# Attention values summed one key tile at a time, and feed-forward weights folded from quarter pieces

## The chip, the core and the metric

The kernel runs on one NeuronCore of a Trainium2 chip. The metric is the device time of one execution in microseconds. Five engines run their own instruction streams and meet only at semaphores: PE (TensorE, matrix products), DVE (VectorE), ACT (ScalarE), POOL (GpSimd) and SP (here only a queue that issues DMAs). The profile lists the weight loads of PE apart, as PEld.

## What is computed

The reference is a small residual network over `x` of shape (2, 2048, 256), in four steps, each behind a layer norm:

```python
x = x + attn_a(layernorm(x))   # 44 fixed offsets back in time per token, softmax over them
x = x + ffn(layernorm(x))      # 8 groups of 512 tokens, each with weights of its own
x = x + attn_b(layernorm(x))   # full softmax attention, 16 heads of 16, rotary q and k
x = x + ffn(layernorm(x))      # the same 8 groups again

def ffn(x):                    # no activation between the two products
    h1 = einsum('gmh,goh->gmo', xg, W1) + b1
    return einsum('gmo,gho->gmh', h1, W2) + b2
def attn_b(x):                 # scores = q k^T / 4, attn = softmax(scores), out = attn v
    ...
```

Since nothing stands between the two products of the feed-forward step, W1 (1024x256) and W2 (256x1024) of a group can be multiplied into one 256x256 matrix and b1 into b2, once, and used twice.

## The kernel before

`build` runs four stages one after the other, each a block of its own that ends when all its engines and stores are through.

**fold_ffn (lines 75 to 158)** multiplies the weights of the 8 groups in float32. SP loads whole groups into one of two slots: W1 (1 MB, L102), W2 transposed (1 MB, L103), b1 (L104), b2 (L105); all four count on one semaphore, `loaded[s]`, and a slot is loaded again only when the group before in it is evacuated (`evac`, L101). PE waits for `loaded[s]`, does 16 products of 128x128 by 128x256 (two row blocks m, eight key blocks k; two records each, L118) and then, when DVE has weighted and summed W2 by b1 in eight steps (L134, L136), one product with a column of ones (L121). DVE copies the result out (L144, L145), and ACT stores it to `mt_d` and `bc_d` (L153, L154). Behind the loop ACT stores one more group into the unused place 0 (L156, L157) and waits for all stores. Every engine runs this as a loop of 4 turns with two slots in each.

**local_stage (lines 337 to 868)** is everything up to the queries, keys and values of attn_b. The change doesn't touch it.

**full_attention (lines 871 to 1193)** takes 4 heads and 512 queries at a time: 2 batches x 4 head groups x 4 query chunks make `ITERS` = 32 iterations. In iteration x PE computes transposed scores of 16 key tiles of 128 keys (`score`, L1047; 4 heads, so 64 scores of 128x512, n = 4 x tile + head). Each goes to one of 3 PSUM banks, in turn; ACT takes the exponential from there into `pr` (L1132), which holds 4 key tiles. A score waits until the exponential of the score three before is done (`bank_free`). PE then multiplies `pr` with the values (`weigh`, L1057): for a key tile 4 products of 128x32 by 128x512 in float32, one per head in its own 32 columns of the array, which run side by side and have two records each.

The exponentials need a bound on the scores of each query, taken one iteration ahead: `max_unit` (L1018) computes 128 queries by 1024 keys into one of two PSUM buffers (two matmuls), DVE takes the maximum (L1149). There are 32 of these units in an iteration; the last 12 of a set are done in the iteration before (`CARRY`). When a set is complete, DVE splits it into three bf16 parts (`max_parts`, L1151 to 1167), PE transposes them into a score bank (`max_rows`, L1027, before score 46), DVE copies them out (L1173) and SP writes them as three extra rows of `qs` (L937).

The order on PE is written out by hand, in pairs of key tiles (`PAIRS` = 8):

```python
for i in range(8):
    score(x, 8 * d + i, q, slot)
    if i in (0, 3, 5, 7):
        fill((0, 3, 5, 7).index(i))
...
weigh((d - 1) % PAIRS, (x - 1) * SCORES + 8 * d)
```

So a pair is 8 scores with 4 units between them, and then the 8 value products of the pair before, in one go. `weigh` counts `pv_done` once a pair. ACT waits for it before it overwrites `pr`; at n == 9 ACT also copies the finished output of the iteration before out of `ps_o` (`take_output`, L1122), and PE waits for this (`o_sb`) at d == 1, before the first value product of the new iteration. POOL waits for `pv_done` before it loads values (`load_v`) and queries and keys (`load_qk`) of later groups. Iterations 1 and 32 stand outside the loop over x, with constant addresses; iteration 32 has no units.

**final_stage (lines 1196 to 1356)** does the rest, chunk by chunk. The change doesn't touch it.

Of the kernel before, what the change touches and what calls it, by code (L numbers as in the profile page):

```python
# [74 lines left out]
def fold_ffn(nc, W1, W2T, b1, b2, mt_d, bc_d):  # L75

    OC = INTER // P
    with ExitStack() as ctx:
        sb = lambda n, s, d: ctx.enter_context(nc.sbuf_tensor(n, s, d))
        sem = lambda n: ctx.enter_context(nc.semaphore(n))  # L80
        w1 = sb("w1", [P, 2, OC, C], F32)
        w2 = sb("w2", [P, 2, OC, C], F32)
        b1s = sb("b1s", [P, 2, OC], F32)
        b2s = sb("b2s", [1, 2, C], F32)
# [5 lines left out]
        loaded = [sem("fold_loaded0"), sem("fold_loaded1")]  # L90
        mm_done, evac, stored = sem("fold_mm"), sem("fold_evac"), sem("fold_stored")
        start, weighted, acc_step = sem("fold_start"), sem("fold_weighted"), sem("fold_acc_step")
        block = ctx.enter_context(nc.Block())

        @block.sync
        def _(sp):
            with sp.Fori(0, NG // 2) as i:
                for s in range(2):
                    g = i * 2 + s

                    sp.wait_ge(evac, i * 2 + s + 1)  # L101
                    sp.dma_start(w1[:, s], W1[g].rearrange("(k p) n -> p k n", p=P)).then_inc(loaded[s], 16)  # L102
                    sp.dma_start(w2[:, s], W2T[g].rearrange("(k p) n -> p k n", p=P)).then_inc(loaded[s], 16)  # L103
                    sp.dma_start(b1s[:, s], b1[g]).then_inc(loaded[s], 16)  # L104
                    sp.dma_start(b2s[:, s], b2[g].unsqueeze(0)).then_inc(loaded[s], 16)  # L105

        @block.tensor
        def _(pe):
            pe.wait_ge(start, 1)
            pe.sem_inc(mm_done, 2)  # L110
            with pe.Fori(0, NG // 2) as i:
                for s in range(2):
                    pe.wait_ge(loaded[s], i * 64 + 64)

                    pe.wait_ge(evac, i * 2 + s + 1)
                    for m in range(KC):
                        for k in range(OC):
                            pe.matmul(ps[:, s, m, 0:C], w1[:, s, k, m * P:(m + 1) * P], w2[:, s, k, :],  # L118
                                      start=(k == 0), stop=(k == OC - 1))
                    pe.wait_ge(weighted, i * 2 + s + 1)  # L120
                    pe.matmul(ps[0:1, s, 2, 0:C], column[:, :], acc[:, s, :], start=True, stop=True).then_inc(mm_done, 1)  # L121

        @block.vector
        def _(dve):
            dve.memset(column[:, :], 1.0).then_inc(start, 1)
            dve.sem_inc(evac, 2)
            dve.sem_inc(stored, 64)
            with dve.Fori(0, NG // 2) as i:
                for s in range(2):

                    dve.wait_ge(loaded[s], i * 64 + 64)
                    for k in range(OC):
                        if k == 0:
                            step = dve.tensor_scalar(acc[:, s, :], w2[:, s, k, :], b1s[:, s, k:k + 1], None, ALU.mult)  # L134
                        else:
                            step = dve.scalar_tensor_tensor(out=acc[:, s, :], in0=w2[:, s, k, :], scalar=b1s[:, s, k:k + 1],  # L136
                                                            in1=acc[:, s, :], op0=ALU.mult, op1=ALU.add)
                        if k < OC - 1:
                            step.then_inc(acc_step, 1)
                            dve.wait_ge(acc_step, (i * 2 + s) * (OC - 1) + (k + 1))  # L140
                    step.then_inc(weighted, 1)
                    dve.wait_ge(mm_done, i * 2 + s + 3)
                    dve.wait_ge(stored, i * 64 + 64)
                    dve.tensor_copy(mt[:, s], ps[:, s, 0:KC, 0:C])  # L144
                    dve.tensor_tensor(bc[:, s], ps[0:1, s, 2, 0:C], b2s[:, s], ALU.add).then_inc(evac, 1)  # L145

        @block.scalar
        def _(act):
            with act.Fori(0, NG // 2) as i:
                for s in range(2):  # L150
                    g = i * 2 + s
                    act.wait_ge(evac, i * 2 + s + 3)
                    act.dma_start(mt_d[g + 1].rearrange("(k p) n -> p k n", p=P), mt[:, s]).then_inc(stored, 16)  # L153
                    act.dma_start(bc_d[g + 1].unsqueeze(0), bc[:, s]).then_inc(stored, 16)  # L154
# [3 lines left out]
            act.wait_ge(stored, 64 + 32 * NG + 32)  # L158
# [712 lines left out]
def full_attention(nc, D):  # L871
# [9 lines left out]
    CARRY = AHEAD * PER_PAIR  # L881
    ROWS_AT = 8 * (PAIRS - AHEAD) + 6
    SCORES = KT * GRP
    QK_LOADS = 16 * 6 * (1 + NCH)

    with ExitStack() as ctx:
        sb = lambda n, s, d: ctx.enter_context(nc.sbuf_tensor(n, s, d))
        sem = lambda n: ctx.enter_context(nc.semaphore(n))
        ps_s = ctx.enter_context(nc.psum_tensor("ps_s", [P, 3, CH], F32))
# [67 lines left out]
        def _(pool):  # L957
# [23 lines left out]
            def group(G, more_qk, more_v):  # L981

                if more_qk:
                    pool.wait_ge(pv_done, G * (NCH * PAIRS) + 1)
                    n = G + 3
                    load_qk(pool.snap(n // HG), pool.snap(n % HG), n)
                if more_v:
                    n = G + 1
                    b, g = pool.snap(n // HG), pool.snap(n % HG)
                    for first, last, loaded in V_LOADS:  # L990
                        pool.wait_ge(pv_done, G * (NCH * PAIRS) + ((NCH - 1) * PAIRS + last // 2))
                        load_v(b, g, first, last, loaded)
# [14 lines left out]
        def _(pe):  # L1007
# [22 lines left out]
            def bank_free(x, op):  # L1030

                if op < 3:
                    last = SCORES + 1 - (2, 1, 3)[op]
                    if not (isinstance(x, int) and x == 1):
                        pe.wait_ge(p_ready, (x - 1) * SCORES + (exps_before(last) + 1 - SCORES))
                elif op - 3 == ROWS_AT:
                    if not (isinstance(x, int) and x == ITERS):
                        pe.wait_ge(nmt_sb, x + 1)
                else:
                    pe.wait_ge(p_ready, (x - 1) * SCORES + (exps_before(op - 3) + 1))  # L1040

            def score(x, n, q, slot):
# [4 lines left out]
                pe.matmul(ps_s[:, op % 3, :],  # L1047
# [4 lines left out]
            def weigh(d, ready):  # L1052

                pe.wait_ge(p_ready, ready)
                for kt in (2 * d, 2 * d + 1):
                    for j in range(GRP):
                        mm = pe.matmul(ps_o[SLOT * j:SLOT * (j + 1), :], vg[:, kt, j, :], pr[:, kt % 4, j, :],  # L1057
                                       start=(kt == 0), stop=(kt == KT - 1), skip_group_check=True)
                mm.then_inc(pv_done, 1)

            def iteration(x, q, slot, group, sets, groups, first=False):

                pe.wait_ge(neg_ld, x * 16)
                for d in range(PAIRS):
                    ahead = d >= PAIRS - AHEAD
                    if sets and d == 0:
                        pe.wait_ge(qk_ready, groups[0])
                    if sets and d == PAIRS - AHEAD:
                        pe.wait_ge(qk_ready, groups[1])

                    def fill(e):
                        if sets:
                            i = PER_PAIR * d + e
# [363 lines left out]
```

## Time and profile before

| | us |
|---|---|
| median of 3 runs (2709.53 to 2711.10) | 2710.88 |
| the profiled execution, its own time | 2717.06 |
| its span in the trace | 2715.4 |
| fold_ffn, from 0 to the first load of local_stage | 93.9 |
| first score of the attention | 1032.2 |
| one iteration of the attention loop | 48.10 |
| last score product ends, last output copied | 2568.5 |

The stages follow each other, so a time saved in one is saved in the whole. Within a stage, the question is which engine's chain of waits sets its length. The page of the profile gives sums over the span; the timeline gives, for a window, each instruction's start and length, with runs of alike instructions merged (x8), and in brackets how long its engine had stood idle and for whom.

### The profile page before, as it was taken

What the parts mean: (1) busy time and instruction counts of PE and PEld (TensorE: products, weight loads), DVE (VectorE), ACT (ScalarE), POOL (GpSimd) and SP (SyncE); (2) the same over time, 40 slices, a digit from 0 to 9 for tenths busy, and PEclk for the clock granted to TensorE, in tenths of its full rate; (3) what the DMA queues carried; (4) which work ended last, traced back from release to release, by engine and by line L of the source; (5) the groups of instructions that cost most, each with busy time, mean ns of one, the idle gap of its engine ahead of it and who ended that gap; (6) DMA issues with size and microseconds to landing.
All of it is one profiled execution on the core that took longest, in us unless ns stands there. A gap on an engine that the chain in (4) does not pass through costs nothing. (4 is left out here: it accounts for less than half of the span.)

```text
span 2715.4 us, 48858 instructions
## 1 busy us (share of the span) xinstructions
PE 2449.6 (90%) x15112; PEld 971.3 (36%) x15112; DVE 2032.7 (75%) x2445; ACT 1418.2 (52%) x2704; POOL 725.0 (27%) x936
## 2 busy tenths in 40 slices
PE   7679999999997559999999999999999999999778
PEld 5334545455545202332333333233333333333144
DVE  4388989999995367787778778787777877877145
ACT  0133434444434105776676677677667767766601
POOL 0488777787772042002002011020000000000010
PEclk9889999999998758999999999999999999999989
DMA  7424444554454295004004013031000000000061
GB/s 220 152 56 120 119 120 120 138 138 118 131 131 132 74 141 64 5 10 59 2 16 52 2 32 36 4 49 17 4 18 4 10 10 4 10 12 2 18 180 44
DMA packets 244299, 174.94 MB, mean 64 GB/s; under 512 B 105172, under 2 KB 215141, under 8 KB 244197
## 3 DMA queue, kind: packets, MB, share of 16 engines
q1 hardware_dynamic: 212406, 116.05, 16.3%
q0 software_dynamic: 13216, 36.72, 9.1%
q10 hardware_dynamic: 18578, 20.85, 2.6%
q8 instruction: 61, 1.00, 0.2%
q14 instruction: 38, 0.31, 0.0%
HBM read 116.49 MB, written 48.31 MB: 61 GB/s over the span
## 5 line engine op out<-in xcount | busy, mean ns | idle before, releaser
L1149 DVE TENSOR_REDUCE mx<-ps_m 128x1 f32<-128x1024 f32 x1036 | 1211.7, 1221 | 327.9 <-PE ps_m L1018 324.6
L1132 ACT ACTIVATE pr<-ps_s 128x512 f32<-128x512 f32 x2048 | 1064.3, 618 | 535.5 <-PE ps_s L1047 520.3
L1047 PE MATMUL ps_s<-qs,ks 99*128 (+1 forms) x2048 | 709.3, 385 | 53.7 <-ACT pr L1132 21.0
L1018 PE MATMUL ps_m<-ks,qs 96*128 (+1 forms) x2072 | 639.0, 391 | 39.6 <-DMA qs<-q_d 33.0
L1057 PE MATMUL ps_o<-pr,vg 128*32 128x512 f32 x4096 | 493.8, 600 | 0.0
L1047 PEld LDWEIGHTS ps_s<-qs,ks 99*128 (+1 forms) x2048 | 196.7, 96 | 715.3 <-issue 619.5
L540 POOL TENSOR_TENSOR prod_p<-qT,kT 128x512 f32<-128x512 f32 x336 | 411.9, 1253 | 108.7 <-PE PSa L583 89.6
L975 POOL DMA_DIRECT2D vg<-vb_d x24 | 19.7, 822 | 1218.8 <-PE ps_o L1057 1211.0
L791 DVE TENSOR_TENSOR prod_d<-PSa,kT 128x512 f32<-128x512 f32 x368 | 232.9, 677 | 24.7 <-PE PSa L583 17.0
L1018 PEld LDWEIGHTS ps_m<-ks,qs 96*128 (+1 forms) x2072 | 180.6, 98 | 176.4 <-DVE mx L1149 44.1
L583 PE MATMUL PSa<-prod_p,sj 128*32 128x512 f32 x672 | 202.9, 618 | 8.7 <-DVE prod_d L791 6.8
L583 PE MATMUL PSa<-prod_d,sj 128*32 128x512 f32 x736 | 203.0, 618 | 8.0 <-DVE prod_d L791 3.1
L1057 PEld LDWEIGHTS ps_o<-pr,vg 128*32 128x32 f32 x4096 | 107.5, 109 | 261.0 <-issue 195.4
L742 ACT COPY a<-PSa 128x512 f32<-128x512 f32 x128 | 68.9, 588 | 185.5 <-PE PSa L641 185.3
L968 POOL DMA_DIRECT2D qs<-q_d x168 | 85.6, 513 | 15.9 <-issue 4.8
L118 PE MATMUL fold_ps<-w 128*128 128x256 f32 x256 | 65.0, 419 | 20.2 <-DMA b2s<-in_b 20.2
L641 PE MATMUL PSa<-ident,own 128*128 128x128 f32 x512 | 70.1, 281 | 6.6 <-DMA prev<-skew 4.1
L588 PE MATMUL PSa<-t_xm,wqkv_b 128*128 128x512 f32 x128 | 69.8, 696 | 5.2 <-DVE rope_b L848 3.6
L641 PEld LDWEIGHTS PSa<-ident,own 128*128 128x128 f32 x512 | 57.8, 143 | 38.6 <-issue 33.7
L555 POOL TENSOR_TENSOR far<-far,fart 128x128 f32<-128x128 f32 x128 | 66.0, 515 | 10.0
L194 ACT ACTIVATE f_sq<-f_xm 128x1024 f32<-128x1024 f32 x8 | 8.5, 1056 | 114.0 <-DVE f_xm L190 114.0
L588 PE MATMUL PSa<-h_xm,wqkv 128*128 128x512 f32 x128 | 65.2, 634 | 2.0 <-DVE h_xm L330 1.3
(134 smaller groups left out, 2073.4 us busy)
## 6 DMA issues: line engine op xcount, KB each, us to landing
own<-skew SPq DMA_DIRECT2D x64, 512.0 KB
ks<-k_d POOLq DMA_DIRECT2D x42, 256.0 KB, 9.3
qs<-q_d POOLq DMA_DIRECT2D x168, 64.0 KB, 9.5
skew<-attn SPq DMA_DIRECT2D x64, 164.0 KB, 4.2
w<-in_W SPq DMA_DIRECT2D x8, 1024.0 KB
w<-in_W2T SPq DMA_DIRECT2D x8, 1024.0 KB
vb_d<-vb SPq DMA_DIRECT2D x8, 1024.0 KB, 5.3
q_d<-qparts ACTq DMA_DIRECT2D x16, 384.0 KB, 2.7
```

The lines of the kernel that those rows point to most:

```text
L540: pool.tensor_tensor(prod_p[:, n % RING, :], qT[:, c, :], kT[:, c, col:col + CH], ALU.mult).then_inc(prod_p_ready, 1)
L583: pe.matmul(PS[SLOT * g:SLOT * (g + 1), SC_BANK, :], sj[:, BANK_J * bank + 4 * g + r, :], rhs[:, n % RING, :], start=(r == 0), stop=(r == ...
L588: mm = pe.matmul(out, weight[:, k, :], x[:, k, :], start=(k == 0), stop=(k == KC - 1))
L641: tr = pe.transpose(PS[:, TURN_BANK[half], h * P:(h + 1) * P], own[:, w % 2, 4 * half + h, :], ident[:, :])
L742: act.copy(a0[:, 4 * half:4 * half + 4, :], PS[:, TURN_BANK[half], :].rearrange("p (h t) -> p h t", h=4)).then_inc(turn_sb, 1)
L791: dve.tensor_tensor(prod_d[:, n % RING, :], PS[:, Q_BANK[c], :], kT[:, c, col:col + CH], ALU.mult).then_inc(prod_d_ready, 1)
L968: pool.dma_start(qs[r, bass.ds(g * NCH + n, 1), :, :].rearrange("p a j t -> p (a j) t"), D["q_d"][Q_STACK[i], :, heads, bass.ds(b * T + (1 ...
L1018: mm = pe.matmul(ps_m[:, u % 2, kc * CH:(kc + 1) * CH], qs[0:KROWS, bass.ds(nq, 1), j, qt * P:(qt + 1) * P].rearrange("p a t -> p (a t)"), ...
L1047: pe.matmul(ps_s[:, op % 3, :], ks[:, bass.ds(slot, 1), j, kt * P:(kt + 1) * P].rearrange("p a t -> p (a t)"), qs[:, bass.ds(q, 1), j, :]. ...
L1057: mm = pe.matmul(ps_o[SLOT * j:SLOT * (j + 1), :], vg[:, kt, j, :], pr[:, kt % 4, j, :], start=(kt == 0), stop=(kt == KT - 1), skip_group_ ...
L1132: act.activation(pr[:, n // GRP % 4, n % GRP, :], ps_s[:, op % 3, :], ACT.Exp, scale=HD ** -0.5).then_inc(p_ready, 1)
L1149: dve.tensor_reduce(mx[:, j * TILES + qt, half:half + 1], ps_m[:, u % 2, :], AX_X, ALU.max).then_inc(m_read, 1)
```

## The change

In `fold_ffn` the loops are written out and the weights arrive in pieces of a quarter group (2 of the 8 key blocks of W1 and of W2, 256 KB each). There are 8 places for pieces, each with its own semaphore. PE starts a group with its first piece; a place is loaded again when PE and DVE are both done with the piece in it. b1 and b2 of all groups are loaded once, behind the second piece, on a semaphore for DVE alone. DVE sums the weighting of group g before it copies group g - 1 out. The additional store into place 0 is gone.

```diff
+    PIECES = 4
+    KP = OC // PIECES
+    DEPTH = 8
@@ sync
+                if i >= DEPTH:
+                    sp.wait_ge(piece_used, i - DEPTH + 1)
+                    sp.wait_ge(weighted, i - DEPTH + 1)
+                sp.dma_start(w1[:, n], W1[g, rows, :].rearrange("(k p) n -> p k n", p=P)).then_inc(w_ld[n], 16)
+                sp.dma_start(w2[:, n], W2T[g, rows, :].rearrange("(k p) n -> p k n", p=P)).then_inc(w_ld[n], 16)
+            for i in range(NG * PIECES):
+                piece(i)
+                if i == 1:
+                    sp.dma_start(b1s[:, :, :], b1.rearrange("g p k -> p g k"), allow_slow_non_contiguous=True).then_inc(b_ld, 16)
+                    sp.dma_start(b2s[:, :, :], b2.unsqueeze(0)).then_inc(b_ld, 16)
@@ tensor
+            for g in range(NG):
+                s = g % 2
+                if g >= 2:
+                    pe.wait_ge(evac, g - 1)
+                for q in range(PIECES):
+                    i = g * PIECES + q
+                    n = i % DEPTH
+                    pe.wait_ge(w_ld[n], 32 * (i // DEPTH + 1))
                     for m in range(KC):
+                        for k in range(KP):
+                            mm = pe.matmul(ps[:, s, m, 0:C], w1[:, n, k, m * P:(m + 1) * P], w2[:, n, k, :],
+                                           start=(q == 0 and k == 0), stop=(q == PIECES - 1 and k == KP - 1))
+                    mm.then_inc(piece_used, 1)
+                pe.wait_ge(acc_ready, g + 1)
+                pe.matmul(ps[0:1, s, 2, 0:C], column[:, :], acc[:, s, :], start=True, stop=True).then_inc(mm_done, 1)
@@ vector
+                dve.sem_inc(acc_ready, 1)
+                if g:
+                    output(g - 1)
+            output(NG - 1)
@@ scalar
-            act.dma_start(mt_d[0].rearrange("(k p) n -> p k n", p=P), mt[:, 1]).then_inc(stored, 16)
-            act.dma_start(bc_d[0].unsqueeze(0), bc[:, 1]).then_inc(stored, 16)
```

In `full_attention` the unit of the written order is one key tile instead of a pair: 4 scores, with a unit behind the first and the third, and then the 4 value products of the tile before. `pv_done` counts tiles, and all waits for it are rewritten to match (POOL's loads too). `CARRY` (12 units) and `ROWS_AT` (46) keep their values, and there are still 3 score banks and 4 tiles of `pr`. The output copy moves from behind exponential 9 to behind exponential 4.

```diff
-    PAIRS = KT // 2
-    PER_PAIR = MAXU // PAIRS
-    AHEAD = 3
+    PER_TILE = MAXU // KT
+    AHEAD = 6
+    SB = 3
+    FILL_AFTER = (0, 2)
@@ tensor
-            def weigh(d, ready):
+            def weigh(kt, ready):
 
                 pe.wait_ge(p_ready, ready)
-                for kt in (2 * d, 2 * d + 1):
+                for j in range(GRP):
+                    mm = pe.matmul(ps_o[SLOT * j:SLOT * (j + 1), :], vg[:, kt, j, :], pr[:, kt % 4, j, :],
+                                   start=(kt == 0), stop=(kt == KT - 1), skip_group_check=True)
+                mm.then_inc(pv_done, 1)
@@ iteration
+                for kt in range(KT):
+                    ahead = kt >= KT - AHEAD
                     for j in range(GRP):
+                        score(x, GRP * kt + j, q, slot)
+                        if sets and j in FILL_AFTER:
+                            e = PER_TILE * kt + FILL_AFTER.index(j)
+                            max_unit((CARRY + e) % MAXU, x * MAXU + (CARRY + e), *sets[ahead])
+                        if sets and GRP * kt + j + 1 == ROWS_AT:
                             bank_free(x, ROWS_AT)
+                            max_rows(x, ROWS_AT % SB)
+                    if kt == 1:
                         pe.wait_ge(va_ld, group * 16 + 16)
                         if not first:
                             pe.wait_ge(o_sb, x - 1)
+                    weigh((kt - 1) % KT, (x - 1) * SCORES + GRP * kt)
@@ scalar
+                for kt in range(KT):
+                    if not (first and kt < 4):
+                        act.wait_ge(pv_done, y * KT + (kt - 3))
+                    for j in range(GRP):
+                        n = GRP * kt + j
-                        if n == 9 and not first:
+                        if n == 4 and not first:
                             take_output(y - 1)
```

## Rows read from the trace of the kernel before

**Rows 1.** The page: busy time of the engines, packets of DMA queue 1

```profile
PE 2449.6 (90%) x15112; PEld 971.3 (36%) x15112; DVE 2032.7 (75%) x2445; ACT 1418.2 (52%) x2704; POOL 725.0 (27%) x936
...
q1 hardware_dynamic: 212406, 116.05, 16.3%
```

**Rows 2.** Timeline of the attention loop, one pair, PE: start us, length us, instruction

```profile
1500.40 0.39 PE L1047 MATMUL ps_s<-qs,ks 99*128 x1
...
1501.57 0.39 PE L1047 MATMUL ps_s<-qs,ks 99*128 x1
...
1502.22 0.38 PE L1047 MATMUL ps_s<-qs,ks 99*128 x1
...
1503.69 0.39 PE L1047 MATMUL ps_s<-qs,ks 99*128 x1
...
1504.13 0.38 PE L1018 MATMUL ps_m<-ks,qs 96*128 x1
1504.44 0.64 PE L1057 MATMUL ps_o<-pr,vg 128*32 128x512 f32 x4
1504.89 0.61 PE L1057 MATMUL ps_o<-pr,vg 128*32 128x512 f32 x4
...
1505.75 0.61 PE L1057 MATMUL ps_o<-pr,vg 128*32 128x512 f32 x4
1506.30 0.39 PE L1047 MATMUL ps_s<-qs,ks 99*128 x1
```

**Rows 3.** The same pair on ACT and DVE, brackets: idle before

```profile
1500.83 0.60 ACT L1132 ACTIVATE pr<-ps_s 128x512 f32<-128x512 f32 x1 [2.01 <-PE ps_s L1047]
1501.48 0.60 ACT L1132 ACTIVATE pr<-ps_s 128x512 f32<-128x512 f32 x1
...
1503.41 0.63 ACT L1132 ACTIVATE pr<-ps_s 128x512 f32<-128x512 f32 x1
...
1506.72 0.60 ACT L1132 ACTIVATE pr<-ps_s 128x512 f32<-128x512 f32 x1 [1.71 <-PE ps_s L1047]
1501.27 1.23 DVE L1149 TENSOR_REDUCE mx<-ps_m 128x1 f32<-128x1024 f32 x1 [1.39 <-PE ps_m L1018]
```

**Rows 4.** Timeline of one loop iteration: output copies, value products of pairs 0 and 1

```profile
1086.75 0.58 ACT L1122 COPY ou<-ps_o 128x512 f32<-128x512 f32 x1
...
1134.85 0.58 ACT L1122 COPY ou<-ps_o 128x512 f32<-128x512 f32 x1
...
1516.22 1.92 PE L1057 MATMUL ps_o<-pr,vg 128*32 128x512 f32 x16
1522.60 1.92 PE L1057 MATMUL ps_o<-pr,vg 128*32 128x512 f32 x16
```

**Rows 5.** Timeline of the last iteration, without units, constant addresses

```profile
2522.28 0.82 PE L1047 MATMUL ps_s<-qs,ks 99*128 99x512 bf16 x3
...
2523.36 2.35 PE L1047 MATMUL ps_s<-qs,ks 99*128 99x512 bf16 x5 [0.26 <-ACT pr L1132]
...
2531.53 3.38 PE L1057 MATMUL ps_o<-pr,vg 128*32 128x512 f32 x16
...
2568.46 0.58 ACT L1122 COPY ou<-ps_o 128x512 f32<-128x512 f32 x1 [2.61 <-PE ps_o L1057]
```

**Rows 6.** Timeline of the weight folding; its last line opens the next stage

```profile
10.24 9.75 PE L118 MATMUL fold_ps<-w 128*128 128x256 f32 x32 [10.24 <-DMA b2s<-in_b]
...
20.43 7.17 PE L118 MATMUL fold_ps<-w 128*128 128x256 f32 x32
...
31.44 8.86 PE L118 MATMUL fold_ps<-w 128*128 128x256 f32 x32 [3.31 <-DMA b2s<-in_b]
...
88.51 0.59 PE L121 MATMUL fold_ps<-acc,column 128*1 128x256 f32 x2
...
93.87 0.39 SPq L431 DMA_DIRECT2D xh<-in_xT  x1
```

**Rows 7.** DMA by slices of 2.5 us, from 0 to 100 us

```profile
GB/s 9 267 358 339 349 340 20 0 0 157 385 360 185 384 365 56 0 105 385 365 193 379 368 98 0 83 362 370 188 365 377 148 0 105 0 0 143 75 256 372
```

More of the change, by code:

```diff
@@ L96, in _, with piece @@
         def _(sp):
[L97 to L105, printed above, removed]
+            def piece(i):
+                g, k = i // PIECES, i % PIECES * KP
+                n = i % DEPTH
+                rows = slice(k * P, (k + KP) * P)
+                if i >= DEPTH:
[3 more added lines that the diff above has]
+                sp.dma_start(w2[:, n], W2T[g, rows, :].rearrange("(k p) n -> p k n", p=P)).then_inc(w_ld[n], 16)
@@ L107, in _ @@
+            for i in range(NG * PIECES):
[3 more added lines that the diff above has]
+                    sp.dma_start(b2s[:, :, :], b2.unsqueeze(0)).then_inc(b_ld, 16)
         @block.tensor
         def _(pe):
[L109 to L115, printed above, removed]
-                    for m in range(KC):
[L117 to L121, printed above, removed]
+            pe.wait_ge(filled, 1)
@@ L123, in _ @@
         @block.vector
         def _(dve):
[L125 to L145, printed above, removed]
@@ new lines, in _, with output @@
+            dve.memset(column[:, :], 1.0).then_inc(filled, 1)
+            def output(g):
+                s = g % 2
+                dve.wait_ge(mm_done, g + 1)
+                if g >= 2:
+                    dve.wait_ge(stored[s], 32 * (g // 2))
+                dve.tensor_copy(mt[:, s], ps[:, s, 0:KC, 0:C])
+                dve.tensor_tensor(bc[:, s], ps[0:1, s, 2, 0:C], b2s[:, g], ALU.add).then_inc(evac, 1)
+            dve.wait_ge(b_ld, 32)
+            for g in range(NG):
+                s = g % 2
+                if g >= 2:
+                    dve.wait_ge(mm_done, g - 1)
+                for k in range(OC):
+                    i = g * PIECES + k // KP
+                    if k % KP == 0:
+                        dve.wait_ge(w_ld[i % DEPTH], 32 * (i // DEPTH + 1))
+                    if k:
+                        dve.wait_ge(acc_step, g * OC + k)
+                    w = w2[:, i % DEPTH, k % KP, :]
+                    if k == 0:
+                        step = dve.tensor_scalar(acc[:, s, :], w, b1s[:, g, k:k + 1], None, ALU.mult)
+                    else:
+                        step = dve.scalar_tensor_tensor(out=acc[:, s, :], in0=w, scalar=b1s[:, g, k:k + 1], in1=acc[:, s, :],
+                                                        op0=ALU.mult, op1=ALU.add)
+                    step.then_inc(acc_step, 1)
+                    if k % KP == KP - 1:
+                        dve.wait_ge(acc_step, g * OC + k + 1)
+                        dve.sem_inc(weighted, 1)
+                dve.sem_inc(acc_ready, 1)
+                if g:
+                    output(g - 1)
@@ L1046, in score @@
                 kt, j = n // GRP, n % GRP
-                pe.matmul(ps_s[:, op % 3, :],
+                pe.matmul(ps_s[:, op % SB, :],
                           ks[:, bass.ds(slot, 1), j, kt * P:(kt + 1) * P].rearrange("p a t -> p (a t)"),
```

92 lines of the change are left out of this document (36 added, 56 removed).

## The prediction, made before the changed kernel was run

> **What bounds the kernel now.** I read the page first. PE is busy 90% of the span and ACT 52% [rows 1], which suggests a kernel limited by products, but a matmul's record is longer (0.38 to 0.39 us) than the distance to the next one, so this busy time is no measure of work. The timeline of one pair of key tiles in the attention loop says more. From 1501.57 to 1502.22 four matmuls start in three equal steps, 0.217 us each; that is the real price of a score or a unit matmul, at the higher granted clock [rows 2]. The value products run from 1504.44 to the next score at 1506.30, 1.86 us. The whole pair takes 1506.30 - 1500.40 = 5.90 us. Its 16 slots of 0.217 and the value products make 5.3; the rest is PE waiting. On what, ACT's rows tell [rows 3]. The first exponential of a pair starts 0.43 after its score, the second 0.65 later, the following ones every (1503.41 - 1501.48) / 4 = 0.48. Score 3 starts at 1501.57, which is 0.14 behind the end of the first exponential (1500.83 + 0.60), and score 7 at 1503.69 likewise waits for the fifth. So in the first part of a pair ACT paces PE, through the three banks; in the second part, the value products, only three exponentials are left to do, and ACT then stands idle for 1.71 us. Each engine waits for the other once a pair. DVE is not in it: four maxima of 1.23 at most against 5.90 [rows 2, 3].
>
> One iteration is the distance of two output copies, 48.10 us, against 8 x 5.90 = 47.2. Of the 0.90 on top, 6.38 - 5.90 = 0.48 belongs to pair 1, where ACT does the output copy [rows 4], and the remaining 0.42 to the transposition of the bounds.
>
> In the folding, PE starts a group's products at 10.24, when 2 MB and the two bias loads have landed; a group loaded before is worked off in 7 to 8 us, then PE waits 3.31 us for the next slot, and the products behind that wait take 8.86 instead of 7.17 us, because the granted clock has fallen to its lower level [rows 6]. Transfers run at 340 to 385 GB/s where they run, but stop in between [rows 7].
>
> **The attention, tile by tile.** The new order has per key tile 4 scores, 4 unit matmuls (two units) and 4 value products. What would PE alone need? Seven steps of 0.217 bring it from the first to the last of the eight matmuls; 1504.44 - 1504.13 = 0.31 from that to the first value product; 1504.89 - 1504.44 = 0.45 for the first pass of the four columns; 1506.30 - 1505.75 = 0.55 for the second pass up to the next score [rows 2]. Sum 1.52 + 0.31 + 0.45 + 0.55 = 2.83 us. In this the switch from scores to value products and back costs 0.31 - 0.22 = 0.09 and 0.55 - 0.43 = 0.12, together 0.21, now twice as often.
>
> Does anything hold PE up? With t from the tile's first score, scores stand at 0, 0.65, 0.87 and 1.52 and exponentials at 0.43, 1.08, 1.56 and 2.04, the last ending at 2.67. Score 3 needs the first (1.03 + 0.14 = 1.17, slack 0.35); the next tile's first score at 2.83 needs the second (1.68); its third, at 3.70, the fourth. The value products at 1.83 need the exponentials of the tile before, done by 2.67 - 2.83, that is before this tile began. All waits are met early. DVE has 2 x 1.23 = 2.46 a tile. So PE sets the pace, at 2.83, and ACT (4 x 0.48 = 1.9) no longer stalls it. Two tiles are 5.66 against 5.90.
>
> The output copy: now behind exponential 4, one step ahead of the first value product, which waits for it. Exponential 4 starts at 0.43, the copy at 0.91 and ends at 1.49, before 1.83; the exponentials behind it end by 3.0, and the score that needs the last of them stands at 3.70. Its 0.48 vanishes. Bound: 0 to 0.5. The transposition keeps a slot on PE: I take 0.3 of its 0.42. DVE's five small steps on the bound fit into the 0.37 us a tile that it has left, over a few tiles; two PSUM buffers stand between it and PE. The SP store of the rows has some 4.5 tiles, 12.7 us, as before. POOL's loads wait for counts of the same meaning and have whole iterations of time: nothing.
>
> An iteration becomes 16 x 2.83 + 0.3 = 45.6, 2.5 less than 48.10. Thirty iterations of the loop: -75. The first, partly at the lower clock and without output copy: between 0 and 2.5, I take -1. The last has no units, so that ACT sets the pace: score 3 starts 2523.36 - 2522.28 = 1.08 after the first [rows 5], then 0.32 + 0.45 + 0.55 gives 2.40 a tile. Sixteen, and a last value product that waits for the last exponential (2.67 + 0.1 + 1.05 in place of 2.40): 36.0 + 3.8 = 39.8, and 0.2 for a copy that is just too late for the first value product, 40.0 against 2568.46 - 2522.28 = 46.2. Of the 46.2, 1.5 is one value product at the lower clock (3.38 instead of 1.92) [rows 4, 5], which may come back. I take -5.5, between -4 and -6.2. Together -81.5.
>
> **The folding by quarters.** The first piece is 0.52 MB. From 2.5 to 5 us 267 GB/s were moved, so it has landed near 4.5 [rows 7]; a completed load was noticed about 1 us later (the slices sum to 2.1 MB by some 9.1 us, PE started at 10.24), so PE starts at about 5.3. It is then not starved: a piece takes 0.52 MB / 350 GB/s = 1.5 us to load and 7.17 / 4 = 1.8 us to multiply. b1 as a whole is 1024 rows of 32 bytes; at the mean packet of queue 1 (16.3% x 16 x 2715.4 / 212406 = 33 ns) [rows 1], 64 on each DMA engine cost 2.1 us, between pieces 1 and 2, while PE works at the lower clock. DVE can weight group 0 from about 10, needs 4, and PE wants the sum at 5.3 + 9.75 = 15.0: hidden, or up to 2 us late. The first group takes 20.43 - 10.24 = 10.2 with its time at the lower clock, the others 7.6 (7.17, and 0.45 around the product with the ones). PE ends at 5.3 + 10.2 + 7 x 7.6 = 68.8 instead of 88.51 + 0.59 = 89.1. Behind it stood 93.87 - 89.1 = 4.8 us of copy, store and wait [rows 6]; without the two additional DMA issues (at the 0.39 of the last row) it is 4.0. So the next stage starts at 72.8, -21; bounds -16 (late b1, a longer stretch at the lower clock) and -23.
>
> The other stages are untouched; they shift against the chip's clock gating, for which I allow 2 us either way. **Sum:** -81.5 - 21 = -102.5. The profiled execution took 2717.06 and would take 2614.6; it stands 6.2 above the median of the runs, so against 2710.9 I forecast 2608.4, rounded to 2609. About 0.2%, 5 us, is what a measurement can tell from no change.
>
> **The rivals.** *Waits that are met still cost.* In the loop the waits compare with registers, and score 3 starts 0.14 behind the exponential's end, in the last iteration with constants (2522.28 + 0.43 + 0.60 = 2523.31 against 2523.36) only 0.05 [rows 3, 5]. If 0.09 a tile stays on PE, 16 x 31 x 0.09 = 45 comes back: 2654. For it: a loop iteration has one computed wait more per pair. Against: in the row of four matmuls two have such waits and the steps are still 0.217 [rows 2]. 0.13.
>
> *The attention gains nothing*, because what PE waits for is not what I read, and the turns between ACT and PE merely get shorter: 2710.9 - 21 = 2690. Against it, the slack above. 0.06.
>
> *Switching costs more, and the kernel is slower.* 496 additional switches are in the forecast at 0.21 each. They sit between the last score of a tile and its first value product. If a lone group of four doesn't get its second pass's weights early, and the array drains both times, a switch is dearer; from 102.5 / 496 = 0.21 more, 0.42 in all, the change gives everything back, and at 0.30 more the time is 2609 + 149 = 2758. Against it, the two passes of the first group inside the present block are already 0.45 and 0.43 apart. 0.04.
>
> *Switching costs nothing.* Then a tile is 2.62, the loop gives 0.21 x 16 x 30 = 101 more: 2508. The Trainium skill ("TensorE: Matmul & The Clock Gate", the section "Step-by-step: what each phase is for") says that weight loads are pulled ahead of running matmuls when they go to other row groups or to the background buffer; by that rule the boundaries would be free. The rows of before already contradict it, 0.09 and 0.12 at each boundary [rows 2]. 0.02.
>
> The lower clock in the attention is a smaller matter: it showed where PE had waited for ACT in the last iteration [rows 5], and the new order makes PE wait less. The same page of the Trainium skill ("A second HAM failure mode: psum-queue depth-cycling") names the opposite, a clock that falls when a kernel cycles through PSUM banks with short idle times between groups of matmuls; in the pair shown here, which does just that, the steps are those of the higher clock.
>
> **How the numbers follow.** The forecast, 2595 to 2635 with its own bounds, 0.74; the first rival 0.13, the second 0.06, slower 0.04, free switching 0.02, 0.01 for about equal. The range from 2590 to 2652 takes in the forecast and most of the first rival. Faster by over 0.2%: 0.95; within: 0.01; slower: 0.04.
>
> **What would show it.** Output copies 45.6 apart instead of 48.10; value products in runs of x8, 2.83 apart, 0.31 behind the last score's start and 1.0 ahead of the next score; no wait of a score for ACT in the loop, ACT idle once or twice in every tile in place of 1.71 once a pair; first product of the folding near 5.3, no gap of 3.3 in it, the first load of the next stage near 73. If the copies stand over 46.5 apart, the first place to look is the distance from a value product's start to the next score.

## The result, and the profile after

The changed kernel takes 2613.8 us (median of 4 runs, 2610.64 to 2615.01) against 2711.0 for the kernel before: a ratio of 0.9637 with a 95% interval of 0.9621 to 0.9652, 97 us less. The forecast was 2609, its range 2590 to 2652. The profiled execution took 2615.01 us, with a span of 2613.2.

| stage, us | before | after | difference |
|---|---|---|---|
| fold_ffn, to the first load of the next stage | 93.9 | 71.7 | -22.2 |
| from there to the first unit matmul of the attention | 880.4 | 876.0 | -4.4 |
| first unit matmul to first score | 57.9 | 57.5 | -0.4 |
| first score to the last output copy | 1536.3 | 1460.8 | -75.5 |
| from there to the end of the span | 146.9 | 147.2 | +0.3 |

The sum is -102.2, between two profiled executions of which the one before stood 6 us above its median. Two stages changed, by -97.7 together; the second row is local_stage, whose code is the same.

The timeline of two key tiles in the attention loop after (columns as in [rows 2, 3]):

```profile
1424.02 0.39 PE L1072 MATMUL ps_s<-qs,ks 99*128 x1
1424.24 0.60 PE L1043 MATMUL ps_m<-ks,qs 96*128 x2
1424.44 2.23 ACT L1151 ACTIVATE pr<-ps_s 128x512 f32<-128x512 f32 x4 [0.28 <-PE ps_s L1072]
1424.68 0.59 PE L1072 MATMUL ps_s<-qs,ks 99*128 x2
1424.88 2.36 DVE L1167 TENSOR_REDUCE mx<-ps_m 128x1 f32<-128x1024 f32 x2 [0.48 <-PE ps_m L1043]
1425.11 0.60 PE L1043 MATMUL ps_m<-ks,qs 96*128 x2
...
1425.55 0.38 PE L1072 MATMUL ps_s<-qs,ks 99*128 x1
...
1425.86 1.06 PE L1081 MATMUL ps_o<-pr,vg 128*32 128x512 f32 x8
1426.85 0.39 PE L1072 MATMUL ps_s<-qs,ks 99*128 x1
...
1427.28 2.23 ACT L1151 ACTIVATE pr<-ps_s 128x512 f32<-128x512 f32 x4 [0.61 <-PE ps_s L1072]
```

The tile's scores start at 0, 0.66, about 0.88 and 1.53, its value products at 1.84, the next tile at 2.83. No start is late; the steps are the 0.22 of unhindered matmuls throughout. ACT's four exponentials take 2.23 and then it waits 0.61 for PE, DVE waits 0.48: both now wait for PE in every tile, and PE shows no wait for either. Before, PE waited for ACT at several scores of a pair and ACT for PE during the value products [rows 2, 3].

An iteration, read from the output copies, answers to [rows 4]; with it the value products of two tiles that lie eight apart. The second set of rows shows the tile with the transposition and the first tile of an iteration:

```profile
1376.31 0.58 ACT L1141 COPY ou<-ps_o 128x512 f32<-128x512 f32 x1
1377.23 1.06 PE L1081 MATMUL ps_o<-pr,vg 128*32 128x512 f32 x8
...
1399.91 1.06 PE L1081 MATMUL ps_o<-pr,vg 128*32 128x512 f32 x8
...
1422.10 0.58 ACT L1141 COPY ou<-ps_o 128x512 f32<-128x512 f32 x1
```

```profile
2411.86 0.38 PE L1072 MATMUL ps_s<-qs,ks 99*128 x1
2412.08 0.22 PE L1052 MATMUL ps_s<-identb,nmp 128*128 128x128 bf16 x1
2412.36 0.39 PE L1072 MATMUL ps_s<-qs,ks 99*128 x1
...
1418.22 0.39 PE L1072 MATMUL ps_s<-qs,ks 99*128 x1
1418.57 0.60 PE L1043 MATMUL ps_m<-ks,qs 96*128 x2
```

An iteration takes 45.79 instead of 48.10. A tile is (1399.91 - 1377.23) / 8 = 2.835 long, from the starts of the value products; sixteen are 45.4. The transposition stands between two scores 0.50 apart that were 0.22 apart otherwise: 0.28. The first unit of an iteration follows its score after 0.35 in place of 0.22: 0.13. Why it does so no run settles; the same step is 0.23 in the kernel before and in the runs below with the value products doubled, so it isn't a fixed price of the loop. The tile in which ACT copies the output costs nothing extra.

The folding after, as in [rows 6]:

```profile
5.00 9.07 PE L130 MATMUL fold_ps<-w 128*128 128x256 f32 x32 [5.00 <-DMA w<-in_W2T]
...
14.52 7.17 PE L130 MATMUL fold_ps<-w 128*128 128x256 f32 x32
...
67.39 0.59 PE L134 MATMUL fold_ps<-acc,column 128*1 128x256 f32 x2
...
71.69 0.37 SPq L455 DMA_DIRECT2D xh<-in_xT  x1
```

PE starts 5.2 us earlier, the first group takes 14.52 - 5.00 = 9.5 instead of 10.2, all following ones 7.6 with no gap. Before, three of them had stood behind a wait of 3.3 us for loads and had then run in part at the lower clock; that is 15.2 of the 22.2. The clock shows in a window of the kernel before (busy times of PE, PEld, DVE, ACT and POOL, then the granted clock, here 0.83 on average):

```profile
30.00:40.00 10.00, 8.56 (x32) 7.18 (x32) 3.75 (x8) 0.00 (x0) 0.00 (x0) 0.83 0.78 247
```

For the first group such a window reads 1.00 in both kernels, yet the starts of its matmuls say otherwise: in the changed kernel they are 0.43 us apart up to 8.5 us, which is the step of the stretches granted 0.50, and 0.22 apart from 8.9 us on. The last 1.1 is the end: 71.69 - 67.98 = 3.7 instead of 4.8.

### The profile page after: what moved, and what is told of

Read it like the earlier page. It is cut to its first block and busy times, and to the rows that moved or that the text cites. A ratio compares the mean times of both kernels' runs of the same rounds, so it can differ in the third digit from the quotient of the medians.

```text
span 2613.2 us, 49018 instructions
## 1 busy us (share of the span) xinstructions
PE 2406.7 (92%) x15112; PEld 939.8 (36%) x15112; DVE 2038.7 (78%) x2445; ACT 1468.8 (56%) x2704; POOL 727.3 (28%) x936
## 5 line engine op out<-in xcount | busy, mean ns | idle before, releaser
L1151 ACT ACTIVATE pr<-ps_s 128x512 f32<-128x512 f32 x2048 | 1114.9, 598 | 409.8 <-PE ps_s L1072 385.4
L1081 PE MATMUL ps_o<-pr,vg 128*32 128x512 f32 x4096 | 545.5, 605 | 0.2
L1043 PEld LDWEIGHTS ps_m<-ks,qs 96*128 (+1 forms) x2072 | 198.4, 98 | 252.3 <-issue 44.5
L1081 PEld LDWEIGHTS ps_o<-pr,vg 128*32 128x32 f32 x4096 | 80.6, 107 | 207.2 <-ACT pr L1151 156.7
L755 ACT ACTIVATE sc<-PSa,pbias 128x512 f32<-128x512 f32 (+1 forms) x48 | 33.1, 690 | 56.0 <-PE PSa L607 56.0
```

Of the source, the lines that this page charges most:

```text
L1043: mm = pe.matmul(ps_m[:, u % 2, kc * CH:(kc + 1) * CH], qs[0:KROWS, bass.ds(nq, 1), j, qt * P:(qt + 1) * P].rearrange("p a t -> p (a t)"), ...
L1151: act.activation(pr[:, kt % 4, j, :], ps_s[:, op % SB, :], ACT.Exp, scale=HD ** -0.5).then_inc(p_ready, 1)
```

## The experiments

**The two parts alone.** The folding of after with the attention of before, and the reverse.

```diff
-fold_ffn of before        +fold_ffn of after         (attention of before)
-full_attention of before  +full_attention of after   (folding of before)
```

> The new folding with the attention of before. The changed kernel's trace has the next stage start 22.2 us earlier. Theory (the two parts are independent, the gain of the folding reaches the end): 2711 - 22 = 2689 us, between 2686 and 2692, and output copies in the attention still 48.10 us apart. Rival (the folding's gain is taken back by a later stage, and the attention's part is larger than its own 76 us): about 2700 or more.

> The new attention with the folding of before. Theory: the attention gives 75.5 us by the two traces (first score to last output copy), so 2711 - 76 = 2635 us, between 2632 and 2639, and this run and the one with the folding alone add up to the whole change (97 us) within 3 us. Rival (the parts help or hinder one another): the two gains add up to more than 102 or less than 92 us.

Measured: 2688.9 us (2688.1 to 2690.0) and 2635.8 us (2632.9 to 2639.2), beside 2713.5 for the kernel before in 7 runs on these chips. Ratios 0.991 (0.9894 to 0.9927) and 0.9712 (0.9695 to 0.9728). Against 2711 that is 22 and 75 us, together the 97 of the whole; against the 2713.5 beside them it is 24.7 and 77.7, together 102.4, since the 2.5 us by which those runs of the kernel before were slower count twice. The whole times settle the sum only to that extent; the stages settle it better. With the folding alone, the next stage starts at 71.7 us (as in the whole change) and the attention takes 1537.2 us from first score to last output copy (as before); with the attention alone these are 92.5 (93.9 before) and 1461.0 (1460.8 in the whole change). The iterations are 48.10 and 45.79 us. Each part changes its own stage by the same amount with or without the other, to some 1 us: they are independent.

**More work for ACT, after and before.** One more copy of 128x512 per key tile (of zeros that nobody uses; the lines that set them up are not shown). In the kernel before the condition is `n % GRP == 1`.

```diff
+                        if j == 1:
+                            act.copy(xs[:, 1, :], xs[:, 0, :])
                         if n == 4 and not first:
```

> The changed kernel with one more copy of 128x512 on ACT in every key tile, behind the second exponential; 512 copies of a price of 0.48 us each in a chain. Theory (PE alone sets the pace in the loop, ACT has slack): in the loop the exponentials move to 0.43, 1.08, 2.04 and 2.52 us after the tile's first score, the last ends at 3.12 and is needed at 3.56, so nothing: copies of the output stay 45.8 us apart. Only the last iteration, which ACT paces, gets longer, by 16 x 0.5 = 8 us: 2614 + 8 = 2622 us. Rival (ACT still sets the pace through the three banks, only in shorter turns): 0.48 us a tile, 45.8 + 7.7 = 53.5 us an iteration, some 2860 us.

> The same additional ACT copy, one a key tile, in the kernel before. Theory (in its pairs ACT's chain from the first to the fifth exponential sets when the eighth score can start, and the other one of the two copies falls into the time of the value products): 0.48 us a pair, 5.90 becomes 6.38, an iteration 48.1 + 3.9 = 52.0, total 2711 + 0.48 x 8 x 32 = 2834 us. Rival (ACT paced nothing before either): 2711 us. Second rival (all ACT time counts): 2711 + 0.48 x 512 = 2957 us.

Measured: 2639.0 us after and 2853.3 us before. Output copies with the additional work, after and then before:

```profile
1432.73 0.58 ACT L1144 COPY ou<-ps_o 128x512 f32<-128x512 f32 x1
1479.05 0.58 ACT L1144 COPY ou<-ps_o 128x512 f32<-128x512 f32 x1
```

```profile
1405.05 0.59 ACT L1125 COPY ou<-ps_o 128x512 f32<-128x512 f32 x1
1457.22 0.59 ACT L1125 COPY ou<-ps_o 128x512 f32<-128x512 f32 x1
```

Before, an iteration grows by 52.17 - 48.10 = 4.07 us, 0.51 a pair, near the 0.48 expected. Over all it is 142 us rather than the 123 expected. Between the two profiled executions the attention grows by 136: 122 from the first to the thirty-first output copy, 4.5 ahead of them and 9.4 behind, where a loop iteration grows by 4.1. The other 6 us are the distance of the profiled execution before from its median. After, it grows by 0.53 in all, not by 7.7. The rival is out: the same 16 copies cost nearly eight times less. But I had expected 0, and 2622 us in all, 17 less than measured. The 0.53 sits in one place, the first tile of an iteration:

```profile
1427.57 1.09 ACT L1154 ACTIVATE pr<-ps_s 128x512 f32<-128x512 f32 x2
1428.65 0.39 PE L1074 MATMUL ps_s<-qs,ks 99*128 x1 [0.25 <-ACT pr L1154]
```

There the first score waits for ACT and comes 0.32 late, and the unit behind it, 0.55 after the score in place of 0.35, adds 0.20 whose cause stays open. The banks explain the wait: 64 scores and one transposition are 65 uses of 3 banks, and 65 is not a multiple of 3, so at the turn the first score gets the bank of the score two before it instead of three (`bank_free`, `op` < 3). In the changed kernel this wait is met in time; with one more copy on ACT it isn't. The other miss is the last iteration, for which I had expected 8 us: from the thirty-first output copy to the last it grows from 36.99 to 38.76, 1.8 us. ACT had still been idle 0.33 us in each of its tiles, so it isn't paced by ACT alone. Together with the stretch ahead of the first output copy (1.9) the attention grows by 18.8 us; the rest of the 25 lies in the other stages and ahead of the first score, which differ by as much between other runs.

**Grain or places?** With the tile order the units move too, behind every second score. Pairs with the units there (shown against the attention of before; the folding is the new one, and the output copy stays behind exponential 9):

```diff
-                        if i in (0, 3, 5, 7):
-                            fill((0, 3, 5, 7).index(i))
+                        if i in (0, 2, 4, 6):
+                            fill((0, 2, 4, 6).index(i))
```

> The new folding with the attention in pairs, as before, but with its units behind scores 0, 2, 4 and 6, which is where the tile order has them. Theory (the grain of the value products gives the gain, the units' places don't): in a pair the third unit waits for DVE to empty its PSUM buffer (2.22 us in place of 2.0) and the fourth likewise (3.36), and the eighth score stands behind it, so a pair takes 5.97 us where the old order takes 5.87 by the same reckoning, 0.1 more: iterations of about 48.8 us, 2689 + 25 = 2714 us in all. Rival (the even spread of units took PE's waits away, with pairs or without): iterations of 45.8 to 46.3 us, about 2615 to 2630 us.

Measured: 2675.8 us, in between, and faster than the same kernel with the old places (2688.9), where I had expected slower. One pair of it, and its output copies:

```profile
1432.16 0.39 PE L1071 MATMUL ps_s<-qs,ks 99*128 x1
...
1434.39 0.60 PE L1042 MATMUL ps_m<-ks,qs 96*128 x2
...
1435.44 0.60 PE L1042 MATMUL ps_m<-ks,qs 96*128 x2
...
1436.19 1.92 PE L1081 MATMUL ps_o<-pr,vg 128*32 128x512 f32 x16
1438.05 0.39 PE L1071 MATMUL ps_s<-qs,ks 99*128 x1
...
1445.50 0.58 ACT L1146 COPY ou<-ps_o 128x512 f32<-128x512 f32 x1
1493.02 0.58 ACT L1146 COPY ou<-ps_o 128x512 f32<-128x512 f32 x1
```

The third unit waits for DVE where expected (2.23), the fourth at 3.28 rather than 3.36, and the pair takes 5.88 to 5.89, practically the old 5.90. An iteration takes 47.52, because the pairs with the output copy and with the transposition now cost 0.23 more than the others (6.11) instead of 0.48. So of the 2.31 us an iteration that the attention gained, the places of the units alone give 0.58; the grain of the value products, with the new place of the output copy, gives the other 1.73 on top of them. This split holds in this order only. Taken the other way round it is different: the next run, with the grain of tiles and nearly the old places, gains only 0.81, and the places then give 1.50. The two work together.

**One unit moved by one place**, in the changed kernel.

```diff
-    FILL_AFTER = (0, 2)
+    FILL_AFTER = (0, 3)
```

> The changed kernel with the second unit of a tile behind its fourth score instead of its third: the same instructions, one pair of matmuls moved by one place. Theory (PE's pace holds only where a score comes late enough for its bank): now the fourth score comes at 1.08 us of a tile and has to wait for the first exponential, 0.43 + 0.60 + 0.14 = 1.17, which costs 0.09 us a tile: 2.92 instead of 2.84, an iteration 47.1 us, in all 2614 + 42 = 2656 us. Rival (the price of a tile is the sum of PE's work and switches in whatever order): 45.8 us, 2614 us.

Measured: 2663.3 us, with output copies 47.29 us apart. Same instructions, 1.5 us more an iteration (1.3 expected): the order decides whether PE's pace holds. A regular tile takes 2.91, so 0.08 more and not 0.09; the tile with the transposition takes 3.56 instead of 3.13, which I hadn't reckoned.

**The price of a switch.** The value products doubled, once in one go and once in two places (`weigh_once` is the old `weigh` with a number for which of the two times it is; `early` holds the waits and the first of the two calls).

```diff
             def weigh(kt, ready):
+                weigh_once(kt, ready, 0)
+                weigh_once(kt, ready, 1)
```

```diff
+                        if j == 1:
+                            early(kt)
...
+                    weigh_once((kt - 1) % KT, (x - 1) * SCORES + GRP * kt, 1)
```

> The changed kernel with the four value products of a tile done twice, directly one behind the other (sums and their divisor both double, so the output stays). Two more passes of 0.43 us and no further switch. Theory (PE sets the pace, a pass is 0.43): a tile takes 2.84 + 0.86 = 3.70 us, an iteration 45.8 + 13.8 = 59.6 us, in all 2614 + 0.86 x 16 x 32 = 3054 us. Rival (ACT has a share in the pace and takes part of it up): less than 0.8 us a tile, under 3020 us.

> The same doubled value products, but the first four behind the tile's second score and the other four behind its fourth: the same work with two more switches a tile (scores to values and back). This prices a switch by itself. Theory (0.09 into the value products and 0.12 out, as in the rows of before): 3.93 us a tile, 0.21 over the run with both in one go, iterations of 63.0 to 63.3 us, in all 3054 + 0.21 x 16 x 32 = 3160 us. Rival of free switching (weights always loaded ahead): the same time as the run in one go. Rival of dear switching (0.42): 3270 us.

Measured: 3048.6 and 3184.6 us. A tile in one go (3.69 us), and one with its value products apart (3.94):

```profile
1431.69 1.92 PE L1082 MATMUL ps_o<-pr,vg 128*32 128x512 f32 x16
...
1435.38 1.92 PE L1082 MATMUL ps_o<-pr,vg 128*32 128x512 f32 x16
```

```profile
1433.86 1.07 PE L1082 MATMUL ps_o<-pr,vg 128*32 128x512 f32 x8
...
1435.83 1.07 PE L1082 MATMUL ps_o<-pr,vg 128*32 128x512 f32 x8
...
1437.80 1.06 PE L1082 MATMUL ps_o<-pr,vg 128*32 128x512 f32 x8
```

A turn from scores to values and back costs 0.24 us (3.938 - 3.694, by the means of the tiles of an iteration), a little over the 0.21 that I had; the first pass of a block takes 0.45 and not 0.43, which I had not counted into the switch. The whole run differs by 136 us, 0.27 for each of 512 tiles, but that holds more than switches: once an iteration the first value products now wait 0.7 us for the output copy, which the run in one go doesn't. Free switching is out, and dear switching too. The Trainium skill ("TensorE: Matmul & The Clock Gate", "Step-by-step: what each phase is for") says that weight loads are pulled ahead of running matmuls when they go to other row groups or to the background buffer; free turns, as that section would lead one to expect, are not what these rows show.

**The place of the output copy.**

```diff
-                        if n == 4 and not first:
+                        if n == 6 and not first:
```

> The changed kernel with the copy of the finished output behind exponential 6 instead of 4. The first value product of an iteration waits for it. Theory (the place behind exponential 4 is what hides the copy): the copy now starts at 1.56 + 0.48 = 2.04 us of the tile and ends at 2.62, with the signal at 2.7, where the value products could start at 1.83; so 0.9 us an iteration: 46.7 instead of 45.8 us, in all 2614 + 0.9 x 31 = 2642 us. Rival (the copy costs nothing anywhere, since it is only one of 65 operations): 45.8 us.

Measured: 2644.5 us, and

```profile
1431.84 0.59 ACT L1141 COPY ou<-ps_o 128x512 f32<-128x512 f32 x1
1478.53 0.59 ACT L1141 COPY ou<-ps_o 128x512 f32<-128x512 f32 x1
```

46.69 an iteration, as expected (46.7); the whole 0.90 lies in the tile of the copy. The copy is free only because of its place.

**The folding: size of a piece, and the clock at its start.**

```diff
-    PIECES = 4
+    PIECES = 2
-    DEPTH = 8
+    DEPTH = 4
```

```diff
+            for n in range(4):
+                pe.matmul(ps[:, 1, 3, 0:C], warm[:, 0:P], warm[:, :], start=True, stop=True)
             for g in range(NG):
```

(`warm` is a tile of zeros that DVE has written; those lines are not shown.)

> The changed kernel folding from halves of a group in 4 places instead of quarters in 8, with the same memory. Theory (the size of a piece only sets how early PE can start; behind that PE is the bound either way): the first piece is twice as large, 0.5 MB more at 0.35 MB/us is 1.5 us, so the first product starts near 6.5 instead of 5.0 us and the next stage near 73.2 instead of 71.7 us. Rival (the small pieces are what keeps PE fed all through the stage): gaps between groups come back and the next stage starts at 78 us or later.

> The changed kernel with four products of zeros, into a PSUM bank that nothing reads, in the time in which PE waits for the first piece (1.2 to 4.6 us at the lower clock). Theory (the first group takes 9.07 instead of 7.17 us because the granted clock is at its lower level when the products start, and activity before them lifts it earlier): the first group takes 7.2 to 8.2 us and the next stage starts at 70.0 to 70.9 instead of 71.7 us. Rival (the first group is slow because its pieces arrive slowly): 9.0 us as before, 71.7 us.

```profile
6.12 8.53 PE L130 MATMUL fold_ps<-w 128*128 128x256 f32 x32 [6.12 <-DMA w<-in_W2T]
...
73.05 0.37 SPq L455 DMA_DIRECT2D xh<-in_xT  x1
```

```profile
1.34 3.78 PE L122 MATMUL fold_ps<-warm 128*128 128x256 f32 x8 [1.34 <-DVE column L142]
...
4.92 7.78 PE L133 MATMUL fold_ps<-w 128*128 128x256 f32 x32
```

Halves start 1.1 us later and end 1.4 later, 73.05; no gap between groups comes back, but PE now waits 0.7 us for DVE's sum in the first group. The 1.4 is one execution against another, and with quarters the same point lay between 71.0 and 72.2 over eight of them; the later start is clear. So small pieces are not what keeps PE fed. Which of the other parts does (a semaphore per piece, reloading before the group is evacuated, the biases loaded once, DVE's new order), no run separates. With products of zeros before it the first group takes 7.78 instead of 9.07 and the next stage starts at 70.31. The matmuls now go over to steps of 0.22 at 6.1 us instead of 8.9: the slow start was the clock. The whole times, 2614.8 and 2608.7, are single runs and don't resolve this.

**Both starts.** The last run adds the same before the first score of the attention.

```diff
+            for n in range(8):
+                pe.matmul(ps_o[:, :], ks[0:KROWS, 0, 0, 0:P], qs[0:KROWS, 0, 0, :], start=True, stop=True)
             pe.wait_ge(nmt_sb, 1)
```

> The changed kernel with products that nothing uses in two waits of PE: the four products of zeros before the first piece of the folding, and eight matmuls into the value bank in the 3.5 us before the first score of the attention, which wait for the first rows of bounds. Theory (both stretches start at the lower clock only because PE was idle before them): the next stage starts at 70.3 instead of 71.7 us, as in the run with the first of the two alone, and from the first score to the first value product it takes 3.6 instead of 5.4 us; together 3.2 us, 2610.6 us. Rival (the eight matmuls delay the first score, because PE is not through when the rows arrive): the first part alone, 2612.4 us or worse. The two cannot be told apart by the whole time, whose untouched middle stage differs by some 8 us between the runs so far; the stretches in the trace decide.

Measured: 2613.7 us (5 runs, 2610.7 to 2616.6), ratio 0.9644 (0.9631 to 0.9657), no different from the changed kernel.

```profile
998.20:1002.00 3.80, 3.64 (x9) 1.06 (x7) 1.49 (x2) 0.00 (x0) 0.00 (x0) 0.50 0.12 19
998.22 3.62 PE L1126 MATMUL ps_o<-qs,ks 96*128 96x512 bf16 x8
1002.12 0.59 PE L1076 MATMUL ps_s<-qs,ks 99*128 99x512 bf16 x1 [0.28 <-issue]
...
1007.52 1.07 PE L1085 MATMUL ps_o<-pr,vg 128*32 128x512 f32 x8
```

The first score was not delayed, but from it to the first value product it still takes 5.40 us, as in the changed kernel. The granted clock was 0.50 during the eight matmuls (first row) and 0.65 over the 5.40 us, as without them. In the folding the gain is there, the next stage starts at 70.5 us; in the attention neither theory held; see the last section.

## Why the prediction was right, point by point

**What bounded the kernel.** Right, and shown from both sides: an additional ACT copy per tile costs the old order 0.51 a pair and the new one nothing in a regular tile.

**A tile at PE's own pace.** 2.83 forecast, 2.835 measured; all its starts lie within 0.02 of those worked out.

**An iteration.** 45.6 forecast, 45.79 measured. Two terms were short: I multiplied 2.83, not 2.835 (0.1 an iteration), and knew nothing of the 0.13 at the turn of the loop. From the first to the thirty-first output copy, thirty iterations, the traces differ by 68.7 us; I had rounded 48.10 - 45.6 to 2.5 and written 75. This is the largest error, 6 us. The transposition (0.3 forecast, 0.28) and the output copy (0) were right, and the copy's place was shown to matter. One reading of before was off without harm: the pair with the transposition is as long as the one with the output copy, 6.38, so 0.48 on top and not 0.42, and a plain pair is 5.89 rather than 5.90.

**First and last iteration.** 6.5 forecast, 75.5 - 68.7 = 6.8 measured. The last one, from its first score to its output copy, takes 40.3 (40.0 forecast) instead of 46.2. Its tiles are 2.40, as worked out, but for two: 2.59 where the output is copied (forecast) and 2.89 for one further on (not forecast), in the place where the other iterations have the transposition:

```profile
2425.67 0.82 PE L1072 MATMUL ps_s<-qs,ks 99*128 99x512 bf16 x3
2426.75 0.39 PE L1072 MATMUL ps_s<-qs,ks 99*128 99x512 bf16 x1 [0.26 <-ACT pr L1151]
2427.07 1.06 PE L1081 MATMUL ps_o<-pr,vg 128*32 128x512 f32 x8
2428.07 0.82 PE L1072 MATMUL ps_s<-qs,ks 99*128 99x512 bf16 x3
...
2465.98 0.59 ACT L1141 COPY ou<-ps_o 128x512 f32<-128x512 f32 x1 [1.19 <-PE ps_o L1081]
```

**The folding.** -21 forecast, -22.2 between the profiled executions. Over all profiled executions the old folding ends at 92.5 to 93.9 (three of them, mean 93.0) and the new one at 71.0 to 72.2 (eight, mean 71.7), so -21.3 is the better number. The old one scatters in part because the clock does not fall behind each of its waits: with the new attention alone, one of the three groups behind a wait took 7.17 and not 8.86. PE's start (5.3; 5.00) and the first group's length at the lower clock (10.2; 9.5) were right within a microsecond. b1 landed in time: DVE began at 7.96 us, and its sum was ready at 12.5, before PE asked at 14.0.

**The sum.** -102.5 forecast against a median difference of 97; the two changed stages give 97.7. The miss of 5 us is the loop's 6, less some 1.5 that the folding and the first and last iteration gave more than forecast. That the two profiled executions are 102.2 apart, as I had written, is chance: they include 4.4 us of the untouched stage.

**The rivals.** Met waits that still cost: out, the starts show none in a tile; the 0.13 once an iteration may or may not be of that kind, no run shows it. Attention without gain: out. Switching dearer by 0.21: out, it costs 0.24 in all, 0.03 more than I had. Free switching: out. The 496 switches of that rival are all lone blocks of four in 31 iterations, and not additional ones, as I had called them; 248 of them are additional. Its times follow from the 496 all the same, since a dearer lone block would be dearer in every tile. What I had not listed is that the places of the units matter by themselves, by 0.58 us an iteration in pairs and 1.50 in tiles (there against nearly the old places). When I did reckon that order, I got its sign wrong: 5.97 for 5.89, where the old order's reckoning, 5.87, had been short by 0.03, and nearly all of the 0.58 lies in the two pairs with the output copy and the transposition, which I hadn't reckoned at all. Differences of 0.1 us in 6 are beyond this way of working.

## What to carry to other kernels

Where two engines feed each other through a few buffers and one also has a block of work that needs no buffer (here the value products), the other starves for the length of that block less what the buffers hold; cut the block until it is shorter than the buffered work, and check that the price of each cut, here 0.24 us for a turn of the array, is less than the wait that it removes. Write out the starts of one period from measured steps before changing an order: one matmul pair moved by one place cost 1.5 us an iteration here. And let the first product wait for as little as it needs. The new pieces took 5 us off the start and all later gaps out. Most of the 5 us is size: half a megabyte more in the first piece costs 1.1 us (6.12 against 5.00), which by an estimate puts a start behind 2 MB at 8.4; only the last 1.9 up to 10.24 are left for the biases on the shared semaphore.

## What the runs showed of the hardware that I had not expected

The untouched local_stage, from its first load to the first unit matmul of the attention, took between 870.5 and 883.7 us over these profiled executions, with the same instructions. In two of them (880.9 and 883.7) the stretch from there to the first score took 54 us instead of 57.5 to 58.9, which gives back a part; up to the first score some 12 us of difference are left. A change of 0.2% in a kernel with such a stage has to be read from stage times.

The clock before the attention's first score rests at the lower level for the whole 53 us of the first units although PE's records fill 84% of them (after every fourth matmul PE waits 0.19 us for DVE). The first row below is this stretch, the second the one from the first score:

```profile
947.70:1001.00 53.30, 44.52 (x88) 6.17 (x89) 50.92 (x49) 0.00 (x0) 15.15 (x30) 0.50 1.00 120
1005.20:1010.60 5.40, 5.37 (x16) 1.92 (x16) 3.40 (x3) 3.45 (x7) 5.01 (x10) 0.65 0.75 101
```

(From the table by windows of the changed kernel: PE, PEld, DVE, ACT and POOL busy, then the granted clock; 0.50 and 1.00 are its two levels.) Eight more matmuls behind these units, 3.62 us long, didn't lift it before the scores. In the folding, 3.8 us of products of zeros did shorten the next stretch, by 1.3 us. What tells the two cases apart stays open; they differ in the type of operands, in what lay before, and in the 0.28 us of idling behind.
